# A decoder block on one core: the row maxima run 7 pairs ahead of the exponentials in place of 13, and their rows travel per half batch

## The reference

```
x = layernorm(x + mixer(x))                      # state-space mixer, 4 heads, chunked scan
x = layernorm(x + attention(q=x, k=v=context))   # 16 heads of 8 channels
x = layernorm(x + experts(x))                    # 8 experts, 2 chosen per token, 128 -> 512 -> 128
# in the attention, per batch and head:
atten = softmax(q @ k.T / sqrt(8));  out = atten @ v
```

## Time and profile before

| what | value |
|---|---|
| three timed executions | 410.9, 411.37, 412.04 us (median 411.37) |
| the profiled execution: its span, first to last instruction | 414.5 us |
| matmuls busy (PE) | 349.5 us, 84% |
| DVE, ACT, POOL busy | 292.3, 235.2, 230.4 us |
| mean granted TensorE clock | 0.980 |

### The profile page before, as it was taken

One profiled execution on the slowest core, in us unless ns is written; L12 is line 12 of the kernel. 1 busy time (PEld: TensorE's weight loads), 2 busy tenths in 40 slices (PEclk: granted clock), 3 DMA queues, 4 the chain that ended last, 5 costly groups with the idle time before them and its releaser, 6 DMA issues.

```text
span 414.5 us, 9020 instructions
## 1 busy us (share of the span) xinstructions
PE 349.5 (84%) x2869; PEld 238.0 (57%) x2869; DVE 292.3 (71%) x836; ACT 235.2 (57%) x460; POOL 230.4 (56%) x341
## 2 busy tenths in 40 slices
...
GB/s 269 336 110 106 87 85 77 187 94 186 171 33 166 5 140 5 99 70 75 196 69 131 117 155 102 74 32 40 53 41 78 78 53 40 53 52 35 32 171 146
DMA packets 44461, 41.97 MB, mean 101 GB/s; under 512 B 4560, under 2 KB 38416, under 8 KB 44416
## 3 DMA queue, kind: packets, MB, share of 16 engines
...
...
## 4 chain that ended last, share of the span: by engine, by line
PE 56%; DVE 20%; issue 7%; POOL 7%; ACT 4%; another core or an unknown queue 3%; DMA 2%; ACTq 0%; DVEq 0%; POOLq 0%
PE banks L1017 12%; DVE nm L1210 8%; PE banks L1044 6%; PE banks L1032 4%; PE banks L859 4%; PE banks L698 4%; PE banks L907 3%; PE banks L1045 2%; PE banks L755 2%; PE banks L937 2%; PE banks L763 2%; DVE ctx_in L1152 2%; PE banks L806 2%; PE banks L934 1%
## 5 line engine op out<-in xcount | busy, mean ns | idle before, releaser
L1210 DVE TENSOR_REDUCE nm<-banks 128x4 f32<-128x1024 f32 x64 | 78.1, 1220 | 17.5 <-PE banks L850 11.4
L1520 ACT ACTIVATE probs_all<-banks 128x1024 f32<-128x1024 f32 x64 | 65.4, 1023 | 36.0 <-PE banks L859 29.6
L1017 PE MATMUL banks<-w_split,scores_in 128*128 x234 | 64.5, 410 | 0.0
L1342 DVE TENSOR_TENSOR ctx_in<-ctx_in,banks 128x512 f32<-128x512 f32 x39 | 26.8, 687 | 27.3 <-ACT ctx_in L1567 21.4
L1017 PEld LDWEIGHTS banks<-w_split,scores_in 128*128 128x128 f32 x234 | 40.8, 189 | 7.7 <-issue 0.9
L1705 POOL DMA_INDIRECT slots_dram<-rows,place_u x32 | 31.9, 996 | 23.5 <-DVE count L1302 16.1
L1727 POOL DMA_INDIRECT y_dram<-x,scatter_u x39 | 38.5, 987 | 11.4 <-POOL x L1723 9.7
L1567 ACT ACTIVATE ctx_in<-banks 128x512 f32<-128x512 f32 x39 | 23.3, 599 | 36.7 <-PE banks L1017 31.9
L859 PE MATMUL banks<-scores_in 32*128 32x256 f32 x256 | 32.2, 326 | 12.0 <-ACT probs_all L1520 6.0
L1044 PE MATMUL banks<-w_split,scores_in 128*128 x156 | 39.1, 327 | 2.8 <-ACT scores_in L1573 2.1
L907 PE MATMUL banks<-probs_all,vals 128*9 128x256 f32 x512 | 39.7, 381 | 0.2
...
## 6 DMA issues: line engine op xcount, KB each, us to landing
...
ctx_in<-in_L_ffn_w SPq DMA_DIRECT2D x16, 256.0 KB, 2.7
cs_wide<-cs_dram SPq DMA_DIRECT2D x14, 256.0 KB, 3.7
...
k_dram<-split_qk SPq DMA_DIRECT2D x8, 256.0 KB, 2.5
q_dram<-split_qk SPq DMA_DIRECT2D x8, 256.0 KB, 2.3
ctx_in<-in_L_ffn_wo SPq DMA_DIRECT2D x8, 256.0 KB, 2.9
```

Of the source, the lines that this page charges most:

```text
L1017: m = TE.matmul(up_bank(i, j), xT[:, i % XT, xh, :], all_weights[:, c + j * FF:][:, bass.ds(expert_at[i], FF)], start=n == 0, stop=n == 2)
L1210: V.tensor_reduce(most, maxima_of(n).rearrange("p (j k q) -> p j k q", j=2, k=TPS), AX_X, ALU.max, negate=True).then_inc(s["nmax"], 1)
L1520: C.activation(probs(n).rearrange("p j k q -> p (j k q)"), EXPS, ACT.Exp, scale=SCALE).then_inc(s["probs"], 1)
```

## The change

LEAD falls from 13 to 7 and LEADS_IN from 33 to 27, so that mixer and maxima keep their places to each other, and the exponentials, with all that follows them (the attention's tail, the routing), start six steps earlier. The loop has 101 steps in place of 107: steps with maxima alone go from 13 to 7, with both from 51 to 57, with exponentials alone from 13 to 7. The weights are tied to the mixer's end, so they now start at step 44; the last eight pieces go two to a step in steps 60 to 63. The maxima travel in 16 groups of four pairs, 16 rows each; a group is split in the step of its last maximum, turned and sent in the next step, which is three steps ahead of the first exponentials that need it. The unread matmuls in the mixer's bank move by six steps with the mixer.

```diff
-LEAD = 13
+LEAD = 7
+ROWS_OUT = PAIRS_B // 2
+ROW_GROUPS = NPAIR // ROWS_OUT
...
-LEADS_IN = 33
+LEADS_IN = 27
...
-SPLIT_LAG, ROWS_LAG = 0, 3
-UNREAD_IN_MIX = {1: S, 4: S, 5: P, 8: 3 * P, 9: S, 13: 3 * P, 16: 3 * P, 17: 3 * P, 21: S, 24: 3 * P}
+SPLIT_LAG, ROWS_LAG = 0, 1
+UNREAD_IN_MIX = {7: S, 10: S, 11: P, 14: 3 * P, 15: S, 19: 3 * P, 22: 3 * P, 23: 3 * P, 27: S, 30: 3 * P}
...
-            b, late = divmod(n + LEAD + 1 - lag, PAIRS_B)
-            if not late and 1 <= b <= B:
-                yield stage, b - 1
+            g, late = divmod(n + LEAD + 1 - lag, ROWS_OUT)
+            if not late and 1 <= g <= ROW_GROUPS:
+                yield stage, g - 1
...
-        elif n >= LAST_MIXER + 6 and piece < PIECES:
-            yield "split_weights", piece
-            if W_RING <= piece + 2 < PIECES:
-                yield "load_weights", piece + 2
+        elif n >= LAST_MIXER + 6:
+            for piece in range(piece, min(piece + 1 + (n >= NPAIR - 4), PIECES)):
+                yield "split_weights", piece
+                if W_RING <= piece + 2 < PIECES:
+                    yield "load_weights", piece + 2
             piece += 1
...
-                    b = n // PAIRS_B
-                    q.wait_ge(a[f"mr{b % RING}"], MAX_ROWS * (b // RING + 1))
+                    q.wait_ge(a["mr"], MAX_ROWS * (n // ROWS_OUT + 1))
...
-            def maxima_out(b):
-                q.wait_ge(s["nm_split"], 2 * (b + 1))
+            def maxima_out(g):
+                q.wait_ge(s["nm_split"], 2 * (g + 1))
                 misc.wait()
...
-                    m = TE.transpose(MISC[0:2 * AH, k * P:(k + 1) * P],
+                    m = TE.transpose(MISC[0:AH, k * P:(k + 1) * P],
...
-                misc.freed_at(s["nm_out"], b + 1)
+                misc.freed_at(s["nm_out"], g + 1)
```

More of the change, by code:

```diff
@@ L377, in build @@
         nm = sb("nm", [P, 2, TPS, AH])
-        nm_parts = sb("nm_parts", [P, TPS, GJ, 2, GR], F32R)
-        nm_rows = sb("nm_rows", [2 * AH, S], F32R)
+        nm_parts = sb("nm_parts", [P, TPS, GJ, 2, GR // 2], F32R)
+        nm_rows = sb("nm_rows", [AH, S], F32R)
         rec = sb("rec", [P, AH])
@@ L513, in sums_turned, with rows_group @@
             return (AV, MISC)[t]
+        def rows_group(g):
+            b, part = divmod(g, 2)
+            return b, slice(part * GR // 2, (part + 1) * GR // 2)
         def second_slot(n):
@@ L613, in load_queries @@
                     SY.dma_start(queries[32 * j:32 * j + 32, r, :, :].bitcast(F32), src).then_inc(a[f"qr{r}"], 16)
-            def maxima_out(b):
-                r = b % RING
-                q.wait_ge(s["nm_out"], b + 1)
-                q.wait_ge(s["nmax"], PAIRS_B * (b + 1))
-                SY.dma_start(queries[3:P:16, r, :, :].bitcast(F32), nm_rows[:, :].bitcast(F32)).then_inc(a[f"mr{r}"], 16)
+            def maxima_out(g):
+                b, rs = rows_group(g)
+                q.wait_ge(s["nm_out"], g + 1)
+                q.wait_ge(s["nmax"], ROWS_OUT * (g + 1))
+                SY.dma_start(queries[3:P:16, b % RING, rs, :].bitcast(F32), nm_rows[:, :].bitcast(F32)).then_inc(a["mr"], 16)
             def sums():
@@ L1208, in maxima @@
                 q.wait_ge(s["max_mm"], n + 1)
-                q.wait_ge(s["nm_split"], 2 * (b - 1))
+                q.wait_ge(s["nm_split"], 4 * (b - 1))
                 V.tensor_reduce(most, maxima_of(n).rearrange("p (j k q) -> p j k q", j=2, k=TPS), AX_X, ALU.max,
@@ L1509, in query, with maxima_out @@
                 C.activation(split_qk[:, slot, 0, :], MIX[:, S:2 * S], ACT.Identity, bias=kv[:, B_Q]).then_inc(s["split_hi"], 1)
-            def maxima_out(b):
-                q.wait_ge(s["nm_t"], b + 1)
-                if b:
-                    q.wait_ge(a[f"mr{(b - 1) % RING}"], MAX_ROWS * ((b - 1) // RING + 1))
-                C.activation(nm_rows[:, :], MISC[0:2 * AH, 0:S], ACT.Identity).then_inc(s["nm_out"], 1)
+            def maxima_out(g):
+                q.wait_ge(s["nm_t"], g + 1)
+                q.wait_ge(a["mr"], MAX_ROWS * g)
+                C.activation(nm_rows[:, :], MISC[0:AH, 0:S], ACT.Identity).then_inc(s["nm_out"], 1)
             def exps(n):
```

10 lines of the change are left out of this document (5 added, 5 removed).

## The result

The changed kernel takes 434.9 us (four executions, 432.88 to 436.16) beside 411.55 us for the kernel before in the same runs (410.9 to 412.04): a ratio of 1.0559, with a 95% interval of 1.0528 to 1.059. The forecast was 415.5 with a range up to 419.5: its sign held, its size missed by 19 us.

What follows compares the result with a forecast made beforehand. PE was taken to carry the step up to 154.00 us, with waits behind that. 0.8 + 3.2 + 7.1 + 1.6 + 5.5 - 14.05 (six removed steps) = +4.2 us, so 411.4 becomes 415.5; 8-in-10 range 406.5 to 419.5.

Steps and rivals of the forecast that it cites:

- Steps 24 to 38: At steps 24 and 32 DVE waits for POOL's `rms` behind four scatters, and PE with it; +7.1 us, up to +9.
- The work of step 27: PE's divide, value product, three unread matmuls and scores in step 27, behind the wait, put at 3.5 us.
- The faster rival: The scatters' new wait lies inside today's stall, so steps 24 to 27 and 32 to 35 keep their times; 406 to 408, chance 0.24.
- The clock's rival: PE's clock falls to 1.2 GHz in three new waits, 1 to 2 us each; +3 to +6, 418 to 421, chance 0.07.
- the lead: Stretch ahead of step 0: steps with two unread matmuls begin six steps earlier in the mixer; +0.8 us, from 0 to 3.8.
- The tail: Steps 57 to 63: the first `up` waits for the last weight pieces behind POOL's own work; +5.5 us, lower end +3.7.
- the ring: The ring of four, in the term for steps 57 to 63, can add 1 to 2 us to the wait for weight pieces.
- Steps 0 to 23: PE carries these steps; its added work nets 2.3 us, plus waits at turns and splits; +3.2 us, from 0 to 5.
- PE's busy share: A sign to look for in the changed kernel's profile: above 88% in steps 0 to 23.
- Steps 39 to 56: At step 53 PE waits for group 14's split, behind batch 3's scatters and four weight pieces on POOL; +1.6 us, 0 to 3.
- Transfers: Sixteen row transfers of 16 KB for eight of 32 KB, costed at nothing; uncovered, up to 0.5 us at each of 16 groups.
- the rival of late rows: Row transfers land after more than three of the fastest steps, delaying every group's exponentials 0.5 us; 8 us more, 423, chance 0.03.

Runs made afterwards that it cites:

- e4: Changed kernel with six unread matmuls on PE at the end of steps 26 and 34, where it idles; 430.1 us, 1.0455 of the kernel before.
- e9: Changed kernel, same order and transfers, with 51 more unread matmuls on PE in the places where it idles; 428.4 us, 1.0412 of the kernel before.
- e2: Changed kernel with the scatters of batches 0 and 1 issued two steps later on POOL; 435.2 us, 1.0575 of the kernel before.
- e11: Changed kernel with the four tile loads on SP in step 62, behind the last weight loads, and their turns in step 63; 433.0 us, 1.0487.
- e7: Changed kernel with the weight pieces two steps earlier; 431.4 us, 1.0504 of the kernel before.
- e8: Changed kernel with a batch's four scatters issued one per step, behind the mixer's operations of four steps; 433.9 us, 1.056 of the kernel before.
- e3: Kernel before with half-batch groups, its lead of 13 kept, PE's turn one step behind POOL's split; 466.3 us, 1.1249 of the kernel before.
- e5: Kernel before with half-batch groups, its lead of 13 kept, PE's turn three steps behind POOL's split; 416.3 us, 1.014 of the kernel before.
- e6: Changed kernel with PE's turn two steps behind POOL's split in place of one; 451.0 us, 1.0946 of the kernel before.
- e12: Kernel before with a lead of 12 in place of 13, turn two steps behind the split in place of three; 1.0289, executions 424.1 to 443.45 us.

## Why the prediction missed, step by step

*Steps 24 to 38, +7.1.* Right in place, cause and size at the clock it assumed: +6.6 and +6.8 in e4 and e9. (The work of step 27 adds up to 3.66 us and not to 3.5, which changes nothing.) The faster rival fell with it: the wait didn't lie inside the one of today.

*The clock's rival, 0.07.* This is the step that failed most. I gave the fall to three waits of 3 us and more, at 1 to 2 us each, since a gap of 2.14 us left the clock up in the earlier trace rows. Six falls came, and some behind 0.9 and 1.35 us of idle time. The gap of the earlier trace rows was a single one, in a stretch where PE worked without a pause for 5 us ahead of it and 10 us behind it, and no other profile has it. That this is what kept the clock up is not shown. The falls cost 5.5 us in the lead, where I had none, and 3.3 us in steps 24 to 38: some 9 of the 15.3 us between +4.2 and +19.5. The other 6.5 are 3.2 in the tail, 1.8 in steps 0 to 23, 1.1 in the lead itself (+1.9 at a clock of 1.00, for +0.8), 0.8 in steps 39 to 56, and -0.4 in steps 24 to 38. The first tile ran at the lower level too, as the rival had it (288.01 to 292.70 us), within the 1.5 us that the expert part lost. Where the falls came in this one profile is in part chance. The Trainium skill ("TensorE: Matmul & The Clock Gate", "Part 1: The HAM clock gate") says that the number of matmuls that one kernel runs ahead of its rise to the full clock changes from run to run. The traces here show as much for falls: e2, e4 and the changed kernel, alike up to step 24, have their first falls in step 8, at the start of step 4 and in step -3.

*The tail, +5.5, measured +8.7.* A term mis-sized. POOL's chain was right (22.7 us to the last piece in e11). That SP issues four tile loads in 4.06 us ahead of the last weight loads I had left out; I cost the ring at nothing in my value, though I named 1 to 2 for it. With the pieces earlier and the clock at 1.00 the tail is +5.0 (e7). It has two nearly equal holders, so that freeing one (e11) shows the other. What the fall of the clock costs there was not separated.

*Steps 0 to 23, +3.2,* measured +5.0 at 0.99: at the upper end given, and +8.2 and +8.3 where a long fall lies in them (e4, e8). PE's busy share is 86% where I looked for over 88. *Steps 39 to 56, +1.6,* measured +2.4, but not where I put it: at step 53 PE waits 0.66 us for the split, at step 49 it waits 1.35, and the clock falls there.

*Transfers.* Right: no wait of the changed kernel goes to the row transfer, and the rival of late rows didn't come. But by costing the groups at their transfers I passed over what a lead of 7 forces on them: the turn one step behind the split. e3 and e5 show that number to be the dearest of the change's parts at a lead of 13; at a lead of 7 it wasn't separated, since with two steps (e6) the turn meets other users of its bank.

What stays open is how the rest, e9's +14.5 against the 4.2 of the forecast, divides between the denser steps and the matmuls that e9 adds. That denser steps cost by themselves is shown at a lead of 12 alone (e12).
